# Scores with a PSUM bank per row tile, and a new order of all turns, in an attention layer with a GRU on one core

## What is computed

```
def attention(x, emb):                       # x: 128 x 32 x 256
    scale, shift = split(emb @ W_emb + b_emb)
    xn = rms_norm(x, g_norm) * (1 + scale) + shift
    q, k, v = heads(xn @ W_qkv)
    q, k = rms_norm(q, g_q), rms_norm(k, g_k)
    o = softmax(q @ k.T / sqrt(16)) @ v
    return o + o @ W_out
def gru(h, x):                               # for each of the 32 tokens
    gi, gh = x_t @ W_ih + b_ih, h @ W_hh + b_hh
    r, z = sigmoid(gi_r + gh_r), sigmoid(gi_z + gh_z)
    n = tanh(gi_n + r * gh_n)
    h = (1 - z) * n + z * h
x = x + attention(x, cond)
x = x + gru(cond, x)
```

## Time and profile before

| | us |
|---|---|
| median of three runs | 350.33 |
| the profiled execution, its own time | 349.93 |
| its span from first to last instruction | 348.1 |
| from the start to S(3) | 38.33 |
| S(3) to S(28) | 138.76 |
| S(28) to the first gate product | 22.75 |
| recurrent part, from the first gate product | 148.26 |

### The profile page before, as it was taken

The page is one execution under the profiler, slowest core; times in us unless marked ns, Lnnn a source line. Parts: engine busy times, 40 slices in busy tenths (PEclk is TensorE's granted clock), DMA queues, the critical chain, the costliest instruction groups (busy, mean ns, idle before and its releaser), DMA issues.

```text
span 348.1 us, 14145 instructions
## 1 busy us (share of the span) xinstructions
PE 331.1 (95%) x5201; PEld 300.5 (86%) x5201; DVE 246.8 (71%) x664; ACT 237.1 (68%) x722; POOL 224.5 (64%) x404
## 2 busy tenths in 40 slices
PE   8989999999999999999998999999999999999994
PEld 8767888878788887878877899999999999999994
DVE  1779988898989889898889555555556555555555
ACT  4788777777777777777755756666666666666663
POOL 6788776676867677686858455555555555555552
PEclk9999999999999999999999999999999999999999
DMA  6961133622111211111111131111111121111111
GB/s 203 312 208 44 30 99 106 189 80 59 58 28 50 62 46 56 29 55 60 54 36 63 39 101 47 57 52 61 59 47 60 60 60 60 60 60 60 60 53 39
DMA packets 26576, 25.81 MB, mean 74 GB/s; under 512 B 3750, under 2 KB 25260, under 8 KB 26540
## 3 DMA queue, kind: packets, MB, share of 16 engines
q1 hardware_dynamic: 24828, 22.10, 20.7%
q10 hardware_dynamic: 1712, 3.21, 3.0%
HBM read 12.46 MB, written 8.39 MB: 60 GB/s over the span
## 4 chain that ended last, share of the span: by engine, by line
PE 87%; POOL 5%; issue 4%; DVE 2%; ACT 1%; POOLq 0%; ACTq 0%; DVEq 0%
PE bank L1233 37%; PE bank L1190 23%; PE bank L1353 8%; PE bank L1334 5%; PE bank L1370 5%; PE bank L1482 2%; PE bank L1317 2%; PE bank L1326 2%; PE bank L1196 2%; POOL wqkv_lo L554 1%; POOL oT_lo L502 1%; POOL xn L476 1%; POOL operands L465 1%; PE bank L1210 1%; POOL wih_lo L495 1%
## 5 line engine op out<-in xcount | busy, mean ns | idle before, releaser
L1233 PE MATMUL bank<-wih_lo,wo_parts 128*128 128x256 f32 x192 | 56.3, 294 | 0.0
L1233 PE MATMUL bank<-wih_hi,wo_parts 128*128 128x256 f32 x192 | 54.5, 285 | 0.2 <-POOL pair_lo L580 0.2
L1233 PE MATMUL bank<-wih_hi,pair_lo 128*128 128x256 f32 x192 | 52.7, 279 | 0.0
L1233 PE MATMUL bank<-wqkv_hi,hT_hi 128*128 128x256 f32 x192 | 52.6, 293 | 0.0
L591 POOL TENSOR_TENSOR operands<-operands,h 128x128 f32<-128x128 f32 x64 | 29.6, 462 | 34.0 <-ACT operands L880 33.2
L1233 PE MATMUL bank<-wqkv_lo,hT_hi 128*128 128x256 f32 x192 | 50.0, 279 | 0.0
L1190 PE MATMUL bank<-wqkv_hi,xn_hi 128*128 128x512 f32 (+1 forms) x124 | 46.5, 375 | 0.2 <-POOL xn_lo L511 0.2
L1133 DVE TENSOR_TENSOR operands<-bank,operands 128x128 f32<-128x128 f32 x64 | 18.6, 291 | 39.4 <-ACT operands L877 39.4
L1233 PE MATMUL bank<-wqkv_hi,hT_lo 128*128 128x256 f32 x192 | 42.7, 279 | 0.0
L598 POOL TENSOR_TENSOR w_emb_sb<-h,w_emb_sb 128x256 f32<-128x256 f32 x31 | 22.9, 737 | 30.7 <-DVE h L1150 30.7
L1190 PE MATMUL bank<-wqkv_lo,xn_hi 128*128 128x512 f32 (+1 forms) x124 | 41.9, 338 | 0.0
(11 more groups left out here) (137 smaller groups left out, 991.8 us busy)
## 6 DMA issues: line engine op xcount, KB each, us to landing
v_diag<-v_rows SPq DMA_DIRECT2D x128, 34.0 KB, 1.9
out_dram<-x SPq DMA_DIRECT2D x16, 256.0 KB, 2.2
w_emb_sb<-out_dram SPq DMA_DIRECT2D x32, 128.0 KB, 2.1
out_dram<-w_emb_sb SPq DMA_DIRECT2D x31, 128.0 KB, 1.7
x_in<-in_x_dram SPq DMA_DIRECT2D x7, 512.0 KB, 9.2
stage_w<-in_L_cond_W_ih_dram ACTq DMA_DIRECT2D x2, 384.0 KB, 3.4
w_hh_sb<-in_L_cond_W_hh_dram ACTq DMA_DIRECT2D x2, 384.0 KB, 3.4
w_emb_sb<-in_L_cond_W_emb_dram ACTq DMA_DIRECT2D x1, 512.0 KB, 4.3
```

The source lines that it names most:

```text
L1233: return pe.matmul(dst, moved, gate_columns(weights, k, block), start=False, stop=True, skip_group_check=True)
```

## The change

Four things change together.

1. The scores have four PSUM banks, one for each row tile, and no wait between halves. The four banks (`p_s`, 128 columns of each) are shared: PV's result lies in bank 0, XT's in bank 2, OUT's in bank 3. So the row maximum waits for PV of the turn, OUT and XT wait until the scores have been read, and S waits until o_sb, xmod and the residual have read theirs.
2. All engines have a new order, and the largest lag is 9 in place of 11, so there are 41 turns.
3. The gate weights are loaded by SP in turns 9 to 12 and the biases in turns 7 and 8. Their parts are made in 16 pieces of 192 columns, one in each looped turn, on ACT and on POOL. W_hh has buffers of its own.
4. The special order of late turns is another one: from turn 34 on, DVE transposes o_sb and the probabilities directly behind the division.

```diff
-PE_X2T, PE_V, PE_S, PE_PV, PE_QKT, PE_OUT, PE_XT, PE_QK = 11, 4, 7, 8, 5, 10, 2, 3
+PE_X2T, PE_V, PE_S, PE_PV, PE_QKT, PE_OUT, PE_XT, PE_QK = 9, 4, 6, 7, 5, 8, 2, 3
-POOL_XN, POOL_KEYS, POOL_OT, POOL_XLO, POOL_NEWTON = 3, 6, 10, 3, 1
+POOL_KEYS, POOL_NEWTON, POOL_XN, POOL_OT, POOL_XLO = 5, 1, 2, 7, 2
...
+        p_s = ctx.enter_context(nc.psum_tensor("bank0", [P, 4 * BANK], F32))
+        p_vx2, p_qkT = bank("bank4"), bank("bank5")
+        p_o = p_s[:, P:P + GB * HEADS // 4 * VW]
+        p_xT = p_s[:, 2 * BANK + D:3 * BANK]
+        p_w = p_s[:, 3 * BANK + D:4 * BANK]
...
             def gate_piece(n):
+                hi, whole = (w[:, :, :].rearrange("p m (n f) -> p m n f", n=GATE_PIECES)[:, :, n, :]
+                             for w in (gate_hi, gate_stage))
+                act.copy(hi, whole).then_inc(gate_hi_ready, 1)
...
             def maxima(g, slot):
                 dve.wait_ge(s_ps, g + 1)
+                if later(g, 1):
+                    dve.wait_ge(o_ps, g)
...
             def input_transposes(g, slot):
+                if later(g, PE_S - PE_XT):
+                    pe.wait_ge(logits_ready, g - (PE_S - PE_XT - 1))
...
             def scores(g, slot):
+                if later(g, 2):
+                    pe.wait_ge(o_ready, g - 1)
+                pe.wait_ge(xmod_ready, capped(g, PE_S - PE_XT))
+                if later(g, PE_OUT - PE_S + 1):
+                    pe.wait_ge(x2_ready, g - (PE_OUT - PE_S))
                 pe.sem_inc(scores_clear, 1)
-                for n in range(2):
-                    if n == 1:
-                        pe.wait_ge(s_half, g + 1)
...
+                for c in range(KC):
+                    for b in range(GB):
+                        columns = slice(c * P + T * b, c * P + T * b + T)
+                        for j in range(NB):
+                            rows = slice(PB * j, PB * j + PB)
+                            dst = p_s[T * b:T * b + T, BANK * j + 2 * T * c:BANK * j + 2 * T * c + 2 * T]
...
             def output_projection(g, slot):
-                pe.wait_ge(xmod_ready, capped(g, PE_OUT - PE_XT))
+                pe.wait_ge(logits_ready, capped(g, PE_OUT - PE_S + 1))
...
             def body(base, u):
+                early = isinstance(base, int) and base + u < PE_X2T
...
+                v = group(base, u, PE_V)
+                if v is not None and early:
+                    value_projection(v, (u - PE_V) % 2)
...
+                if v is not None and not early:
+                    value_projection(v, (u - PE_V) % 2)
```

More of the change, by code:

```diff
@@ L48 @@
 FIRST_LOOPED = 16
-GATE_LOADS = 11
-LATE_RESULTS = range(24, 28)
-LAST_TURNS = range(34, 39)
+BIAS_LOADS, GATE_LOADS = 7, 9
+GATE_PIECES = NG - FIRST_LOOPED
+BIAS_SUM = 14
+LAST_TURNS = NG + 2
+SET_GATES = NG + 6
 FIRST_SPREAD = 7
@@ L239, in adaptive_attention_gru @@
         xhat_free = sem("xhat_free")
-        s_half = sem("s_half")
         s_ps = sem("s_ps")
@@ L411, in body @@
                     load_x(4 * FIRST_SPREAD, NG, x_loaded[FIRST_SPREAD])
+                for i in range(4):
+                    if turn_is(base, u, BIAS_LOADS + i // 2):
+                        load_bias(i)
+                    if turn_is(base, u, GATE_LOADS + i):
+                        load_gate_weights(i)
                 o = group(base, u, SP_X2)
@@ L526, in body @@
             def body(base, u):
+                k = group(base, u, POOL_KEYS)
+                if k is not None:
+                    mask_keys(k, (u - POOL_KEYS) % 2)
+                n = norm_item(base, u, POOL_NEWTON)
+                if n is not None:
+                    newton(n, (u - POOL_NEWTON) % 2)
                 g = group(base, u, POOL_XN)
@@ L529, in body @@
                     shift(g, (u - POOL_XN) % 2)
-                k = group(base, u, POOL_KEYS)
-                if k is not None:
-                    mask_keys(k, (u - POOL_KEYS) % 2)
                 if turn_is(base, u, POOL_XLO + 1):
@@ L794, in body @@
             def body(base, u):
+                if turn_is(base, u, FIRST_LOOPED - 1):
+                    for loaded in ih_loaded + hh_loaded:
+                        act.wait_ge(loaded, 16)
+                if turn_is(base, u, SET_GATES):
+                    act.wait_ge(bias_ready, 1)
+                    act.wait_ge(gates_clear[0], 1)
+                    set_gates(0)
+                g = group(base, u, ACT_QKT)
+                if g is not None:
+                    queries_keys(g, (u - ACT_QKT) % 2)
+                v = group(base, u, ACT_V)
+                if v is not None:
+                    values(v, (u - ACT_V) % 4)
                 n = norm_item(base, u, ACT_LN)
@@ L797, in body @@
                     roots(n, (u - ACT_LN) % 2)
-                if turn_is(base, u, NG - 2 + ACT_QKT):
-                    queries_keys(NG - 2, (u - ACT_QKT) % 2)
-                v = group(base, u, ACT_V)
-                if v is not None:
-                    values(v, (u - ACT_V) % 4)
                 if turn_is(base, u, NG - 1 + ACT_X2T):
@@ L808, in body @@
                 d = group(base, u, ACT_X2T)
[L809 to L810 removed]
+                if d is not None:
                     result(d)
[L812 to L814 removed]
                 g = group(base, u, ACT_EXP)
@@ L817, in body @@
                     exponentials(g, (u - ACT_EXP) % 2)
-                for c in range(KC):
-                    if turn_is(base, u, NG + c):
-                        gate_weights(c)
+                if not isinstance(base, int):
+                    gate_piece(base + (u - FIRST_LOOPED))
                 n = group(base, u, ACT_SQX)
@@ L843, in body @@
                     second_squares()
-                for i in range(2 * KC):
-                    if turn_is(base, u, GATE_LOADS + i):
-                        load_gate_weights(i)
                 if turn_is(base, u, ACT_XN):
@@ L1056, in body @@
             def body(base, u):
+                last = isinstance(base, int) and base + u >= LAST_TURNS
                 g = group(base, u, DVE_QKN)
@@ L1069, in body @@
                     shifted_scores(g, (u - DVE_MAX) % 2)
-                if turn_is(base, u, NG - 2 + DVE_QKN):
-                    normalized(NG - 1, (NG - 1) % 2, (NG - 1 + LAG_QK) % 2)
+                g = group(base, u, DVE_SS)
+                if g is not None:
+                    sums_of_squares(g, u % 2)
                 o = group(base, u, DVE_RCP)
@@ L1088, in body @@
                     last_low_part((u - DVE_OT) % 2)
-                o = group(base, u, DVE_O)
-                if o is not None and not late_residual:
-                    attention_output(o, (u - DVE_O) % 2)
+                g = group(base, u, DVE_XMOD)
+                if g is not None:
+                    modulated(g, (u - DVE_XMOD) % 2)
                 g = group(base, u, DVE_PT)
-                if g is not None and not late_residual:
+                if g is not None and not last:
                     probs_transposed(g, (u - DVE_PT) % 2)
+                o = group(base, u, DVE_OT)
+                if o is not None and not last:
+                    attention_transposed(o, (u - DVE_OT) % 2)
                 if turn_is(base, u, 0):
```

212 lines of the change are left out of this document (74 added, 138 removed).

## The result

The change makes the kernel **slower: 364.96 us** (median of 4 runs, 363.49 to 365.58) against 350.42 us (349.92 to 351.29), a ratio of 1.0406 with a 95% interval of 1.0366 to 1.0447. The forecast of 351.4 us had the sign right and the size wrong; its range ended at 355.5. The sign is partly luck: the steady turns, forecast to save 5.3 us, lost 2.6. The profiled execution took 365.49 us, with a span of 363.7 against 348.1.

| stretch | before, us | forecast | after, us | measured |
|---|---|---|---|---|
| start to S(3) | 38.33 | -0.7 | 40.45 | +2.1 |
| S(3) to S(28), 25 turns | 138.76 | -5.3 | 141.32 | +2.6 |
| S(28) to first gate product | 22.75 | +7.0 | 33.49 | +10.7 |
| recurrent part | 148.26 | 0 | 148.44 | +0.2 |

A forecast was written before the change was run, and what follows sets the result against it. The prediction took PE to set the attention part's turn of 5.54 us. Fill -0.7, steady turns -5.3 and drain +7.0 summed to +1.0 us, giving 351.4 us, with a range of 345.0 to 355.5.

The forecast's parts named there:

- the steady turns: The 25 turns from S(3) to S(28): 5.33 us each, 0.21 less than before, so -5.3 us in all.
- The scores: Score passes S on PE: without the wait between halves, S up to PV takes 0.62 us, 0.46 less.
- Rival (a): Score passes: the four row tiles overlap, 64 passes in the time of 32, S 0.39 us, total 345.0; chance 0.13.
- The new wait: Shared score banks: OUT can start 2.20 us after PV starts, PE gets there at 1.95, idle 0.25 us a turn.
- QKT: Transposes of q and k on PE, between PV and OUT in a steady turn: taken as 0.41 us.
- The pieces and SP's queue: Gate-weight pieces on ACT and POOL are covered by idle time; DMA issues moved to SP's queue cost 0.
- Rival (c): Steady turns: the DVE and ACT cycle, or POOL with its pieces, becomes the bound; turn 5.55, total 356.7 us; chance 0.14.
- Rival (d): Scores: row tiles sharing columns run one after the other, S stays 1.08 us, new wait on top, 364.3; chance 0.03.
- The fill: Start to S(3): shorter pipeline, bank waits, earlier OUT, shorter S and DVE's output weights sum to -0.7 us.
- the pipeline is one turn shorter: In the fill, up to S of group 3: one turn fewer, saving 4.62 us.
- The drain: From S(28) to the first gate product: 29.8 us instead of 22.75, so +7.0 us, bounds +4 and +9.
- Rival (b): Drain: if EXP is not held behind logarithm and x2T copy, two intervals lose 1.5 us each, total 348.4; chance 0.12.

## Why the prediction was wrong, point by point

**The scores: the term was mis-sized.** "They are issued over 0.45 - 0.22 = 0.23 us", so S 0.62. The spread of the recorded starts is not the pace: the 0.39 us from the second half to PV was, and twice 0.39 is the 0.78 measured. This is 0.16 us a turn, 4.0 over 25 turns. The 0.39 stood in the earlier trace rows, and the prediction used it for the second half alone. Rival (a) fell with it: the Trainium skill, "TensorEngine Tiling (Array Packing)", section "Theoretical Speedup", gives 32-row tiles up to four times the rate, and here two and four row tiles ran at the same 12.2 ns a pass.

**The new wait: right in kind, its path too short.** Row maximum behind PV, OUT behind the subtraction, PE idle for 0.30 us against 0.25 forecast. But from PV to OUT, "0.68 + 0.06 + 0.72 + 0.69 + 0.05 = 2.20", it is 2.34 us (137.38 to 139.72): DVE follows PV after 0.13 us, not 0.06, and PE follows DVE after 0.11, not 0.05. This path sets the turn, so that its 0.14 us come on top, 3.5 in 25 turns. What the Trainium skill, "PSUM — Partial Sum Buffer", section "PSUM bank collisions raise a hardware error", asks for is what the kernel does, and the trace agrees that it costs a wait; a row maximum that does not wait for PV was not tried.

**QKT: mis-sized, at no cost.** It takes 0.49 us with the transposes of X2T behind it, 0.41 with OUT behind it; the prediction carried the 0.41 over. But QKT runs while OUT would wait for DVE, so a longer QKT only shortens the wait. With 0.16 for S and 0.14 for the path from PV to OUT the turn of 5.33 becomes 5.63, and 5.62 was measured; the mean of the 25 turns is 0.03 above that.

**The pieces and SP's queue: right.** No PE wait in a steady turn names POOL or ACT, and moving or removing the pieces changed no turn. Rival (c) did not happen. Rival (d) did not either: S is shorter, and the run with the wait put back shows by how much, 0.30 us a turn. That its 364.3 us lie next to the measured time is chance.

**The fill: wrong sign.** The bank waits of 0.85, 0.76 and 1.07 us are there, 2.7 in all against 3.54 forecast. Two other steps failed. The first is "the pipeline is one turn shorter: less 4.62 us". That is the length of a turn with S and PV in it, but as many S and PV stand ahead of S(3) as before; the turn that is saved lies ahead of S(0) and has neither. S(0) starts 3.17 us earlier, here before and after:

```profile
24.94 0.45 PE L1353 MATMUL bank<-operands,qkT 32*32 32x64 f32 x32
```

```profile
21.77 0.85 PE L1333 MATMUL bank<-k_masked,qkT 32*32 32x64 f32 x64
```

The second is "some 2 us, half of it covered, 1.0": of DVE's output weights (26.48 to 28.94) 1.47 us became a wait of PE, and behind the waits the granted clock was at half from 30.5 to 33.9, some 1.3 us more, which the sum put at nothing. The three S save 0.9 instead of 1.38. So the terms are off by 1.45 + 0.47 + 1.3 + 0.48 - 0.86 = 2.8 us, which is the difference. Moving the output weights alone gave 1.7.

**The drain: right in kind, too small.** The intervals from S(28) on are 7.30, 6.86, 7.69, 5.05 and 6.59 us against 7.15, 6.49, 5.38, 4.39 and 6.36. The order did what was forecast (QKT(30) ahead of S(29), the residual behind probsT and qkn(31)). The step that failed is S(30) to S(31), 2.3 us too short, where PE ran at half clock; with the clock at full it took 5.85. The prediction used durations at 2.4 GHz for a stretch in which it had itself put long waits on PE. The other intervals are 1.4 us too short together. Rival (b) asked for a drain shorter by EXP's place, which was not tried; QKT(30) and the residual turned out to be an order that counts.

**The sum.** +1.0 forecast, +15.6 measured: 7.9 of the difference in the steady turns, 3.7 in the drain, 2.8 in the fill, 0.2 in the recurrent part. The remark behind it, that the steady turns save what the drain gives back, failed at the steady turns first.

## What to carry to other kernels

Read the pace of short passes from the start of a group to the start of the next instruction on the engine, not from the spread of recorded starts, and check it on a group that nothing interrupts. A bank that two stages share turns an order that was free into a wait; look for a product that writes elsewhere and put it ahead of the step that waits. Where an edit makes PE wait in a fill or a drain, price its rows at both clocks, and look at what stands ahead of the waited-for step on the other engine's queue.

## What the runs showed of the hardware that was not expected

- 64 passes of 32 rows by 64 columns on four row tiles took 0.78 us, 32 on two took 0.39, in either order. The weight loads of such passes are on PE's load side for 105 ns each, 21.8 us in all for 32 groups, 0.68 us of each S; that they set the pace is argued only:

```profile
L1333 PEld LDWEIGHTS bank<-k_masked,qkT 32*32 32x32 f32 x2048 | 21.8, 105 | 14.5 <-issue 12.9
```

- A wait for a count that is worked out in registers takes time on the waiting engine's queue (57 to 82 ns for one such instruction on DVE). It shows as "issue", and counts only where nothing else covers it.
- PE's granted clock fell to 1.2 GHz within an idle time of 2.80 us, behind others of 0.57 and 1.21, and came back 10 us later; it fell behind an idle time of 1.25 in the same place too, for a shorter time; with 16 unread products in that place it stayed at 2.4 GHz there and fell behind a later wait. In the fill the same fall came in some executions and not in others, behind the same waits, for 1.3 us of S(1) to S(2) (8.10 against 6.82).
